# Experts chosen batch by batch with token numbers scattered into a DRAM list, and the mask bias taken in through feature 0 of the normed rows

## The reference, cut to what matters

```python
# attention over 64 context rows, 16 heads of 64, mask and top 32
h = layernorm(x)                                   # over the 256 features
scores = einsum(h @ Wq * inv_temp, ctx @ Wk) / sqrt(64)
scores = where(mem_mask, scores, -inf)
attn = softmax(scores) * (scores >= top_k(scores, 32)[..., -1:])
x = x + (attn / (attn.sum(-1) + 1e-8)) @ (ctx @ Wv) @ Wo
# self-attention over 512 rows, 16 heads of 16
y = layernorm(x)
hn = layernorm(y) * ln1_g + ln1_b
y = y + softmax(q @ k.T / 4) @ v @ wo + bo
# experts: each row takes the one with the largest logit (the first of equals)
hn2 = layernorm(y) * ln2_g + ln2_b
idx = argmax(hn2 @ gate_w + gate_b)
out = x + y + relu(hn2 @ w1[idx] + b1[idx]) @ w2[idx] + b2[idx]
```

## Time and profile before

| | us |
|---|---|
| median of three runs | 1403.3 (1400.73 to 1408.4) |
| the profiled execution | 1396.75 |
| its span, first to last instruction | 1394.9 |
| last gate logits of the attention part end | 1051.9 |
| first expert matmul starts | 1090.9 |
| PE busy in the span | 1283.2 (92%) |
| DVE busy | 942.8 (68%) |
| ACT busy | 854.2 (61%) |
| POOL busy | 682.3 (49%) |

### The profile page before, as it was taken

How to read it: one execution, slowest core, us unless ns; L and a number is a source line. 1 busy time by engine, 2 the same in 40 slices (tenths; PEclk the granted TensorE clock), 3 DMA queues, 4 the chain that set the end, 5 groups by cost and what they waited for, 6 DMA issues and landing times. The chain is left out here.

```text
span 1394.9 us, 27066 instructions
## 1 busy us (share of the span) xinstructions
PE 1283.2 (92%) x7138; PEld 922.0 (66%) x7138; DVE 942.8 (68%) x6185; ACT 854.2 (61%) x2061; POOL 682.3 (49%) x816
## 2 busy tenths in 40 slices
PE   7868799999999999999999999999972899999996
PEld 5445576577576566656757666655531799989996
DVE  3887987996997998799699789944426122222221
ACT  2334488697878879779787887977860122222221
POOL 2557453555356355445624734632013466666673
PEclk9989999999999999999999999999995899999998
DMA  5210641743363184175337417418513264385551
GB/s 189 83 62 9 167 93 31 169 99 77 101 154 82 55 181 93 40 154 121 77 91 155 91 33 196 78 49 195 93 46 136 77 221 152 82 303 187 188 193 26
DMA packets 105009, 161.43 MB, mean 116 GB/s; under 512 B 35058, under 2 KB 58232, under 8 KB 100760
## 3 DMA queue, kind: packets, MB, share of 16 engines
q1 hardware_dynamic: 86760, 106.51, 32.7%
q0 software_dynamic: 18096, 53.19, 11.7%
HBM read 161.81 MB, written 46.53 MB: 149 GB/s over the span
## 5 line engine op out<-in xcount | busy, mean ns | idle before, releaser
L1013 ACT ACTIVATE pt<-fr 128x512 f32<-128x512 f32 x512 | 277.1, 617 | 25.7 <-PE fr L613 22.6
L1244 DVE CUSTOM_DVE_ANT_0 over<-fr,over 128x256 f32<-128x256 f32 x512 | 197.8, 418 | 86.7 <-ACT over L1023 79.2
L1023 ACT ACTIVATE over<-fr 128x256 f32<-128x256 f32 x512 | 179.0, 391 | 53.4 <-PE fr L613 49.0
L613 PE MATMUL fr<-qs,ks 128*128 128x512 f32 x512 | 189.1, 452 | 3.8 <-DMA qs<-cT 1.3
L613 PE MATMUL fr<-ks,qs 128*128 128x256 f32 x512 | 170.7, 352 | 8.1 <-DVE nmax L1244 3.9
L1358 POOL TENSOR_TENSOR m<-m,e 128x1024 f32<-128x1024 f32 x32 | 75.9, 2371 | 185.0 <-DVE m L1180 185.0
L613 PEld LDWEIGHTS fr<-qs,ks 128*128 128x128 f32 x512 | 87.1, 188 | 86.5 <-issue 50.5
L613 PE MATMUL fr<-kd,qs 128*128 128x256 f32 x512 | 137.5, 283 | 0.0
L814 PE MATMUL ob<-pt,v 128*32 128x512 f32 x1024 | 136.4, 604 | 0.6 <-ACT pt L1013 0.5
L613 PEld LDWEIGHTS fr<-ks,qs 128*128 128x128 f32 x512 | 97.8, 191 | 43.9 <-DVE nmax L1244 25.0
L613 PE MATMUL xs<-VW,pT 128*128 128x256 f32 x512 | 120.2, 389 | 1.8 <-issue 1.7
(11 more groups left out here) (211 smaller groups left out, 2903.9 us busy)
## 6 DMA issues: line engine op xcount, KB each, us to landing
parts_d<-parts SPq DMA_DIRECT2D x32, 512.0 KB, 4.2
ks<-parts_d SPq DMA_DIRECT2D x128, 128.0 KB, 4.0
qs<-parts_d SPq DMA_DIRECT2D x128, 128.0 KB, 4.3
xy_d<-xy SPq DMA_DIRECT2D x32, 256.0 KB, 3.9
kd<-diff_d SPq DMA_DIRECT2D x128, 64.0 KB, 4.1
xyf<-xy_d SPq DMA_DIRECT2D x32, 256.0 KB, 4.0
rows_d<-row SPq DMA_DIRECT2D x32, 256.0 KB, 3.3
diff_d<-diff SPq DMA_DIRECT2D x16, 256.0 KB, 2.3
```

The source lines that it names most:

```text
L613: return pe.matmul(o, l, r, start=first, stop=last)
L1013: act.activation(pt[:, t % 2, h, :], fr_bank(b, "st", 16 * g + n)[:, :], ACT.Exp, scale=D ** -0.5)\
L1023: act.activation(over[:, (16 * g + n + 64 * b) % NREL, :], fr_bank(b, "fs", 16 * g + n)[:, S // 2:S], ACT.Relu)\
L1244: v.tensor_tensor_reduce(rest, fr_bank(b, "fs", 16 * g + n)[:, 0:S // 2], rest, 1.0, -BIG, ALU.add, ALU.max, nmax[:, g % 2, 4 * h + t:4 * ...
```

## The change

It has three parts.

The mask bias goes through feature 0. The normed rows sum to zero over the features, so column 0 of the query weights can be subtracted from the others and cleared without a change of the scores; then feature 0 of every normed row is set to 1, once, and the fold's row 0 holds the bias. DVE subtracts and clears in two halves at the start (`query_weights`, before and after `place_keys`), the first fold of each batch takes a matmul of one row with the bias in each half (16 in all), and the 64 bias matmuls go. `x_norm` writes features 1 to 255.

The experts are chosen batch by batch, inside the attention part. Behind a batch's last logits DVE makes the one-hot rows of its 512 tokens (`choose`, 5 instructions), PE adds up for each token the place in its expert's region of a list (`places`, 5 matmuls in a bank of F), DVE counts on (`count`, 2) and takes the place out (`slots`, 3), and POOL scatters 128 token numbers with each of four DMAs into the list `ids_d` in DRAM (`ids_out`), which SP has filled with the number of an empty row at the start. The second block only makes the table of tiles, on 8 partitions, gathers 39 rows of the list, turns them, and has all row numbers. The table's constants are loaded at the start.

In the experts, the first tile's weights are loaded by SP before the table is known (tile 0 is then always expert 0's), the output bias stands behind the second layer's weights in one row, the indices are read from tables, and the residual is added up behind the first layer's activation instead of ahead of it.

```diff
+    "ch": (331.237,),
+    "dp": (333.413,),
+    "cn": (333.871,),
+    "sx": (335.219,),
+    "ro": (338.117, 339.873, 341.639, 343.291),
...
+REGION = TOK
+RTILES = E * REGION // P + ETILES
+W2COLS = FT * DM + DM
...
+            load(dcon[:, :], dcon_in, dcon_loaded)
+            load(oT[:, :, :].rearrange("p k c -> p (k c)"), pick_in[:, 0:2 * P], dcon_loaded)
+            load(znT[:, 0, 0:E], pick_in[:, 2 * P:2 * P + E], dcon_loaded)
+            load(ids_d[:, :], blank_in, ids_set)
...
                     if b == 0 and c == 0:
-                        pe.wait_ge(wq_loaded, 16)
                         pe.wait_ge(keys_placed, 1)
                     elif c == 0:
                         pe.wait_ge(kbd_loaded, 32 * b)
+                    if b == 0 and c < 2:
+                        pe.wait_ge(wq_ready, c + 1)
                     o = xs_slot(b, "M", c)
                     mt, half = c // 2, c % 2
+                    if mt == 0:
+                        mm(o[:, :].rearrange("p (h c) -> p h c", c=CK), unit[0:1, :],
+                           bias_m[0:1, b * CK:(b + 1) * CK].unsqueeze(1).to_broadcast((1, H // 2, CK)), True, False)
                     for j in range(4):
                         hp = 4 * half + j
-                        ins = mm(o[:, j * P:(j + 1) * P], wqT_s[:, hp, mt * P:(mt + 1) * P], kbd[:, hp, :])
+                        ins = mm(o[:, j * P:(j + 1) * P], wqT_s[:, hp, mt * P:(mt + 1) * P], kbd[:, hp, :], mt > 0, mt > 0 or j == 3)
                     ins.then_inc(xs_full, 1)
...
                     o = xs_slot(b, "sc", 2 * t + half)
-                    mm(o[:, :].rearrange("p (h c) -> p h c", c=CK), top[:, :],
-                       bias_m[:, b * CK:(b + 1) * CK].unsqueeze(1).to_broadcast((P, H // 2, CK)), True, False)
                     if half == 0:
                         xs_read(pe, b, "xt", t)
                     if t == 0:
                         xs_read(pe, b, "M", 2 + half)
                     for k in range(KT):
-                        ins = mm(o[:, :], xnT[:, k, :], M[:, k, half * 512:(half + 1) * 512], False, k == KT - 1)
+                        ins = mm(o[:, :], xnT[:, k, :], M[:, k, half * 512:(half + 1) * 512], k == 0, k == KT - 1)
                     ins.then_inc(xs_full, 1)
...
+            def places(b):
+                yield due(b, "dp")
+                if b == 0:
+                    pe.wait_ge(pick_set, 1)
+                pe.wait_ge(oh_ready, b + 1)
+                wait(pe, acc_ready, b)
+                o = fr_slot(b, "dp", 0)
+                chosen_here = oh[:, :, :].rearrange("p t e -> p (t e)")
+                mm(o[:, 0:NT * E], earlier[:, :], chosen_here, True, False)
+                mm(o[:, 0:NT * E].rearrange("p (t e) -> p t e", e=E), ones[:, :],
+                   acc[:, b % 2, :].unsqueeze(1).to_broadcast((P, NT, E)), False, False)
+                for back in range(1, NT):
+                    ins = mm(o[:, back * E:NT * E], ones[:, :], chosen_here[:, 0:(NT - back) * E], False, back == NT - 1)
+                ins.then_inc(fr_full, 1)
...
-                    copy(xn[:, t % 2, :], x_rows(b)[:, t, :], xr[:, t, 0:1], xr[:, t, 1:2]).then_inc(xn_ready, 1)
+                    copy(xn[:, t % 2, 1:], x_rows(b)[:, t, 1:], xr[:, t, 0:1], xr[:, t, 1:2]).then_inc(xn_ready, 1)
...
+            def query_weights():
+                for part in range(2):
+                    yield due(0, "nh", 0) - 0.02 + 0.015 * part
+                    half = slice(part * HP // 2, (part + 1) * HP // 2)
+                    dve.wait_ge(wq_loaded, 16)
+                    v.tensor_tensor(wqT_s[:, half, 1:], wqT_s[:, half, 1:],
+                                    wqT_s[:, half, 0:1].to_broadcast((P, HP // 2, DM - 1)), ALU.subtract).then_inc(wq_step, 1)
+                    dve.wait_ge(wq_step, part + 1)
+                    v.memset(wqT_s[:, half, 0:1], 0.0).then_inc(wq_ready, 1)
...
-                n = (b * NT + t) * E
-                v.tensor_tensor(logits[:, n:n + E], fr_bank(b, "gt", t)[:, 0:E], gb_b[:, :], ALU.add)\
+                if t == 0:
+                    wait(dve, choice_step, 4 * b)
+                v.tensor_tensor(logits[:, t, :], fr_bank(b, "gt", t)[:, 0:E], gb_b[:, :], ALU.add)\
                  .then_inc(fr_signal(b, "gt", t), 1)
...
+            def choose(b):
+                yield due(b, "ch")
+                wide = (P, NT, E)
+                for t in range(NT):
+                    fr_read(dve, b, "gt", t)
+                v.tensor_reduce(best[:, :], logits[:, :, :], AX.X, ALU.max).then_inc(choice_step, 1)
+                dve.wait_ge(choice_step, 4 * b + 1)
+                v.tensor_tensor(ow[:, :, :], logits[:, :, :], best[:, :].unsqueeze(2).to_broadcast(wide), ALU.is_ge)\
+                 .then_inc(choice_step, 1)
+                dve.wait_ge(choice_step, 4 * b + 2)
+                v.tensor_tensor(ow[:, :, :], ow[:, :, :], dc("order").unsqueeze(1).to_broadcast(wide), ALU.mult)\
+                 .then_inc(choice_step, 1)
+                dve.wait_ge(choice_step, 4 * b + 3)
+                v.tensor_reduce(best[:, :], ow[:, :, :], AX.X, ALU.max).then_inc(choice_step, 1)
+                dve.wait_ge(choice_step, 4 * b + 4)
+                if b > 0:
+                    fr_written(dve, b - 1, "dp", 0)
+                    dve.wait_ge(sum_ready, b)
+                v.tensor_tensor(oh[:, :, :], ow[:, :, :], best[:, :].unsqueeze(2).to_broadcast(wide), ALU.is_equal)\
+                 .then_inc(oh_ready, 1)
+
+            def count(b):
+                yield due(b, "cn")
+                dve.wait_ge(oh_ready, b + 1)
+                wait(dve, acc_ready, b)
+                v.tensor_reduce(tsum[:, :], oh[:, :, :].bitcast(F32).rearrange("p t e -> p e t"), AX.X, ALU.add)\
+                 .then_inc(sum_ready, 1)
+                dve.wait_ge(sum_ready, b + 1)
+                v.tensor_tensor(acc[:, (b + 1) % 2, :], acc[:, b % 2, :].bitcast(F32), tsum[:, :], ALU.add)\
+                 .then_inc(acc_ready, 1)
+
+            def slots(b):
+                yield due(b, "sx")
+                fr_written(dve, b, "dp", 0)
+                v.tensor_tensor(ow[:, :, :], fr_bank(b, "dp", 0)[:, 0:NT * E].rearrange("p (t e) -> p t e", e=E),
+                                oh[:, :, :].bitcast(F32), ALU.mult).then_inc(fr_signal(b, "dp", 0), 1)
+                fr_read(dve, b, "dp", 0)
+                v.tensor_reduce(slot_f[:, :], ow[:, :, :], AX.X, ALU.add).then_inc(slot_ready, 1)
+                dve.wait_ge(slot_ready, b + 1)
+                wait(dve, ids_stored, 16 * NT * b)
+                v.tensor_scalar(slot_i[:, :], slot_f[:, :], 0.0, None, ALU.add).then_inc(slots_ready, 1)
+
+            weave([query_weights(), place_keys(), set_picks()]
+                  + [part(b) for b in range(B) for part in (x_stats, parts_low, choose, count, slots)]
...
+            def ids_out(b):
+                for t in range(NT):
+                    yield due(b, "ro", t)
+                    if b == 0 and t == 0:
+                        pool.wait_ge(ids_set, 16)
+                        pool.wait_ge(dcon_loaded, 16 * 3)
+                    if t == 0:
+                        pool.wait_ge(slots_ready, b + 1)
+                    pool.sem_inc(p_gate, 1)
+                    gp.indirect_dma_start(ids_d.rearrange("r (p o) -> (r p) o", o=1),
+                                          bass.IndirectOffsetOnAxis(slot_i[:, t:t + 1], 0),
+                                          dc("token")[:, b * NT + t:b * NT + t + 1], None,
+                                          bounds_check=E * REGION - 1, oob_is_err=False).then_inc(ids_stored, 16)
+
...
+        def weights_loaded(eng, first, signal, j, q):
+            if q == 0 and j == 0:
+                eng.wait_ge(first, 16)
+            else:
+                eng.wait_ge(signal[q], 16 * (j + q))
+
...
-            sp.dma_start(dcon[:, :], dcon_in).then_inc(dcon_loaded, 16)
+            sp.dma_start(w1s[:, 0, :], w1b[0:P, :]).then_inc(first_w1, 16)
+            sp.dma_start(w2s[:, 0, :], w2t[0:P, :]).then_inc(first_w2, 16)
...
+            settle(v.tensor_scalar(cnt[:, :], counts_at[:, 0:1], of_expert("region"), None, ALU.subtract))
+            settle(v.tensor_scalar(more_than[:, :], of_expert("steps"), cnt[:, 0:1], None, ALU.is_lt))
+            v.tensor_reduce(need[:, :], more_than[:, :], AX.X, ALU.add).then_inc(need_ready, 1)
...
+            dve.wait_ge(need_ready, 1)
+            dve.wait_ge(starts_full, 1)
+            v.tensor_scalar(ends[:, :], starts_at, of_expert("bump"), None, ALU.add)
+            settle(v.tensor_tensor(begins[:, :], starts_at, need[:, :], ALU.subtract))
+            v.tensor_scalar(weigh[:, :], begins[:, :], -float(P), of_expert("region"), ALU.mult, ALU.add)
+            settle(v.tensor_scalar(is_under[:, :], of_expert("tile"), ends[:, :], None, ALU.is_lt))
+            settle(v.scalar_tensor_tensor(chosen[:, :], of_expert("tile"), begins[:, :], is_under[:, :], ALU.is_ge, ALU.mult))
```

(64 more changed lines are left out.)

211 lines of the change are left out of this document (86 added, 125 removed).

## The result

The changed kernel takes 1430.72 us (median of four runs, 1429.73 to 1441.51) where the kernel before takes 1405.85 on the same chip: ratio 1.0192, interval 1.0156 to 1.0228. So it is slower by 24.9 us. Forecast was 1401.9 with a range up to 1416, most likely no change that can be measured. The profiled execution spans 1428.5 us against 1394.9, 33.6 more. Four terms make that up: the attention part up to batch 0's last gate logits +7.3 (298.2 to 305.5), from there to the last batch's +38.9, the hole -8.4, the experts -4.2.

The account below looks back on a forecast made before the run. Three parts, different limits: PE and a nearly full DVE in the attention loop, a serial ladder in the hole. Terms -14.3 + 10.8 + 1.2 + 1.9 + 0.5 - 1.5 = -1.4 gave 1395.35, 1401.9 on the median; range 1388 to 1416.

Parts of the forecast that it names:

- The hole: Last gate logits to first expert matmul, a serial chain of short steps: 14.3 us less, bounds -16 and -10.
- the ladder: Step-by-step times through the hole, from last logits at 1051.88 to first expert matmul at 1074.9, before 1.7 for weight traffic.
- the landing had 4.2 us to hide in: In the hole, the scatters' landing is hidden up to 4.2 us, from 1060.8 to the list gather at 1065.0.
- Above 29, the list landed late: Sign in the hole: above 29 us, against 24 to 25 expected, weight traffic was mis-sized or the list landed late.
- The ten DVE instructions and the bias matmuls: Attention loop, batches 0 to 5: new DVE steps cost 2.3 a batch, dropped bias matmuls give back 0.5; +10.8.
- first rival: The attention part's DVE idling swallows the new DVE work, 0.3 a batch; 1392.0 us, chance 0.22.
- The second: Rival: PE is the bound and its work counts, -5.8 there, -19.7 with start, hole and experts; 1383.6 us, chance 0.08.
- The third: Rival: scatters make GpSimd late in the attention part, 1.7 in six batches, 10.3; 1412.2 us, chance 0.20.
- its sign: Third rival's sign: batch distance 120 or more, with GpSimd's product behind its own scatters and not behind the mask.
- Batch 6 and the last batch: Batch 6 beside the last batch's attention, where DVE is not full: +1.2; batch 7's choosing counts in the hole.
- The start: Before and in the first fold: DVE's query-weight work delays it 1.5, bias rows add 0.4; +1.9.
- The experts: Expert part: GpSimd's bias gather and DVE's index copies go, row gather hangs on the residual; -1.5, bounds -4 and +2.

Follow-up runs that it names:

- last_behind: The changed kernel with the last batch's four id scatters issued behind the boundary between the two parts; 1445.06 us.
- gap_routing: The changed kernel without its bias half, scatters moved ahead of the next batch's first product, the last ones behind the boundary, first weight loads waiting for ids; 1412.6 us.
- bias_alone: The kernel before with only the bias half of the change, experts chosen as before; ratio 1.0054.
- stand_in: The changed kernel with all id scatters behind the boundary and two dummy GpSimd powers at each scatter's old place; 118.3 us a batch.
- pieces64_gap: gap_routing with each id written in a piece of 64 bytes instead of 4; ratio 1.0001 to the kernel before.
- quiet_routing: quiet without the bias half; 8.3 us faster than quiet by the medians.
- quiet: last_behind with the scatters, choosing, counting and slots of batches 0 to 6 moved later, toward supposed idle spells; batch distances 126.4 to 129.4 us.
- run 17: Not a run or kernel: the words belong to "still run 17 us later", a step executing 17 us after its due time.
- plain_writes: The changed kernel, id scatters behind the boundary, plain DMAs of 128 neighbouring 4-byte pieces to a spare tensor at the old places; 125.8 us a batch.

## Why the prediction was wrong, point by point

**The hole (-14.3; measured 30.56 against 39.0: -8.4).** Nearly every step of the ladder held. Choosing to slots took 3.15 (forecast 3.2), the last scatter's issue ended 8.95 behind the logits (8.92), and from the open boundary to the first matmul it was 14.5 (15.5, of it 1.7 for the weights' traffic). The step that failed is "the boundary between the parts cost 0.29", read off from a boundary at which no DMA of GpSimd was under way: it cost 7.1, since the boundary waits until the scatters have landed (0.3 with none under way in last_behind, 2.9 with pieces of 64 bytes). I also said that the landing had 4.2 us to hide in: it had none, because the boundary came first. "Above 29, the list landed late" named the right sign, though I expected the list gather to wait and not the boundary.

**The ten DVE instructions and the bias matmuls (+1.8 a batch, 10.8 in all).** With the scatters away, choosing costs 118.0 - 117.3 = 0.7 a batch, where I had 2.3: mis-sized, between forecast and first rival (gap_routing, without the bias half, has 118.1 against 116.9 in its last three distances: 1.2). The bias matmul was to give back 0.5; bias_alone shows 117.3 against 116.9, so it gives nothing. The sum, 1.1, is near the 1.8 by luck: two wrong sizes that partly cancel. What isn't in it is the other 3.6 a batch (121.52 against 117.95), of which 2.2 are seen as DVE's wait for a late load. The prediction asked of the scatters what they cost GpSimd and when they land, never what they do to transfers of other queues: that term stood at nothing without a reason. That is the step that failed.

**The rivals.** The second (PE's work counts) falls with bias_alone: 48 matmuls fewer, and the distance rose by 0.4. Its sum left out the 0.5 for copying that the first rival has: 1384.1 and not 1383.6. The third forecast 1412.2 through GpSimd's lateness; the side was right, the mechanism wrong (stand_in), and its sign couldn't tell the two apart. Its price was wrong too: 0.57 for each scatter held up beside DVE, where in DVE's full stretch three of a batch's four took 0.99 to 1.24 us and the fourth 1.06 to 1.51, against 0.97 to 1.09 behind the last batch.

**Batch 6 and the last batch (+1.2; measured +4.1 and +11.6).** 6.1 of the last are batch 6's scatters among the last head loads (83.3 against 77.2). The rest, +4.8 and +5.5 over the kernel before, stays in nearly every kernel that chooses batch by batch, with or without scatters; the last batch is shorter only in pieces64_gap (72.9), quiet_routing (74.5), stand_in (75.3) and quiet (76.6). Its cause is not settled.

**The start (+1.9; the first DVE step on scores stands at 32.16 against 27.73: +4.4).** The fold began at 16.23 against 15.00, +1.2, near the delay of 1.5, but by luck: the key placement started only 0.4 late (13.86 against 13.46), because DVE's steps ahead of the new ones stood 0.75 earlier than before, and the bias row, which I had counted behind the delay, added 0.7. The rows below, the time lines of DVE and PE and the stretch table, show the rest.

```profile
13.86 1.39 DVE L1160 TENSOR_TENSOR kbd<-fr,col 64x512 f32<-64x512 f32 x2
...
15.53 0.76 PE L645 MATMUL xs<-bias_m,unit 1*128 1x512 f32 x1 [2.45 <-DVE kbd L1160]
...
25.85 5.37 PE L645 MATMUL xs<-M,xnT 128*128 128x512 f32 x8 [0.52 <-issue]
```

```profile
25.00:31.00 6.00, 5.48 (x10) 2.31 (x11) 0.00 (x0) 1.75 (x4) 0.00 (x0) 0.72 0.01 3
```

A one-row matmul hands over after 0.70 (15.53 to 16.23), not after 0.23 to 0.46. And the first eight score matmuls run partly at the lower level, mean granted clock 0.72, where the kernel before had 1.00 from 22 to 27 us, so they take 5.4 us. Kernels without the bias half have their first mask of batch 0 within 0.7 us of the old one (43.9 us); with it, it stands 2.4 to 6.1 later. By batch 0's last logits the two groups overlap (297.7 to 307.1, and 302.2 to 309.0), so how much of the +7.3 there is the bias half's isn't shown.

**The experts (-1.5; measured 304.0 to 299.8, -4.2).** Right in sign, just past the far bound of -4; bias_alone, with the old experts, has 303.1, the other changed kernels 300.0 to 302.7. PE's late rows behind the first tile come to 7.3 - 4.6 = 2.7 (forecast 3.6).

```profile
PE fr L1678 <- DMA rows<-rows_d,row_table: 7.3, 7, 4.6
```

## What to carry to other kernels

Of every DMA that a change adds, ask what it does to the transfers that fly beside it and to the next point that waits for all of them, not only what it costs its issuer and when it lands. Keep the pieces of a write to DRAM off the size of single words where loads are on a tight loop: here 64 bytes for each id left no slow packet where 4 bytes left 209. And place moved work by the times of the trace, not by the due times of a hand-written order: a step may be due in an idle spell and still run 17 us later.

## What the runs showed of the hardware that I had not expected

512 writes of 4 bytes a batch made packets of the hardware queue, 1 and 2 KB each, take up to 5.4 us in the changed kernel, where the ids are scattered, and up to 6.0 in plain_writes, where the pieces lie in a row (median of the 2 KB packets over the changed run 0.084). With 64 and with 512 bytes a piece it didn't happen (0 and 1 slow packets). The Trainium skill (DMA: Bandwidth & Descriptors, "Specifications") gives 512 bytes as the least piece for full rate, with read-modify-write below it. No run here shows either; the harm to others was gone at 64. The Trainium skill (DMA: Bandwidth & Descriptors, "Back-pressure in remote DMA") says, of transfers between cores, that stalled writes stall the other queues of their engine too. The slow packets look like that on one core, but no run shows inside a DMA engine, so the mechanism is open.

Behind a matmul with one row of weights and 512 columns the next one started 0.42 us later at the full clock (548.64 to 549.06), behind the one with 128 rows and the same columns 0.23 later. The matmuls that follow differ, so how much of the 0.42 is the one row's own isn't shown.
